# Decoder layer with slot attention and experts: another order of work at the beginning and the end of the self-attention

## The reference

```python
qkv = x @ w_qkv + b_qkv                      # 8 x 256 x 768
att = softmax(where(causal, q @ k.T / 4, -inf))
x = layernorm(x + (att @ v) @ w_proj + b_proj)

Pn = rmsnorm(P, input_norm_w); k_proj = Pn @ Wk.T; v_proj = Pn @ Wv.T
for _ in range(3):                           # slots start as x
    scores = rmsnorm(slots) @ Wq.T @ k_proj.T * SCALE
    attn = softmax(scores, axis=-2)          # over the slots
    attn = attn / (sum(attn, axis=-1) + EPS)
    slots = gru_cell(attn @ v_proj, slots)
x = layernorm(x + slots)
x = layernorm(x + experts(x))                # top 4 of 16
```

## Time and profile before

| | us |
|---|---|
| median of 3 runs | 650.16 |
| lowest and highest | 648.36, 651.65 |
| the profiled execution | 649.62 |
| its span, first to last instruction | 647.9 |

### The profile page before, as it was taken

How to read it: one execution, slowest core, us unless ns; L and a number is a source line. 1 busy time by engine, 2 the same in 40 slices (tenths; PEclk the granted TensorE clock), 3 DMA queues, 4 the chain that set the end, 5 groups by cost and what they waited for, 6 DMA issues and landing times.

```text
span 647.9 us, 13973 instructions
## 1 busy us (share of the span) xinstructions
PE 617.4 (95%) x5064; PEld 562.3 (87%) x5080; DVE 492.4 (76%) x1035; ACT 327.7 (51%) x736; POOL 229.9 (35%) x276
## 2 busy tenths in 40 slices
PE   8889999999989899999999999999999999899996
PEld 7667777787779899999999999999988988899895
DVE  5755677666746888979888798897998987867653
ACT  6334655555764456574556645565456646032220
POOL 9703435243453431332313222232313114262442
PEclk9899999999999999999999999999999999999999
DMA  8545476365200400000000000000000000232250
GB/s 302 173 142 171 144 225 179 114 199 177 60 18 1 163 2 2 17 18 1 0 0 16 16 0 0 0 0 0 0 1 2 2 1 1 70 97 92 75 164 32
DMA packets 31710, 43.34 MB, mean 67 GB/s; under 512 B 3408, under 2 KB 19248, under 8 KB 31664
## 3 DMA queue, kind: packets, MB, share of 16 engines
q1 hardware_dynamic: 31392, 42.47, 20.9%
q10 hardware_dynamic: 272, 0.26, 0.1%
HBM read 29.39 MB, written 13.21 MB: 66 GB/s over the span
## 4 chain that ended last, share of the span: by engine, by line
PE 65%; issue 13%; DVE 13%; POOL 5%; ACT 3%; DMA 1%; another core or an unknown queue 0%; DVEq 0%; POOLq 0%; ACTq 0%
PE bank L450 27%; PE bank L2178 11%; PE bank L1990 4%; PE bank L1890 3%; POOL hid_hl L797 3%; PE bank L1848 2%; PE bank L1855 2%; PE bank L1871 2%; PE bank L458 2%; PE bank L2007 2%; PE bank L1976 1%; PE bank L1875 1%; PE bank L1999 1%; PE bank L1857 1%; PE bank L1920 1%
## 5 line engine op out<-in xcount | busy, mean ns | idle before, releaser
L450 PE MATMUL bank<-slots_hl,whhT_hl 128*128 128x256 f32 x864 | 113.4, 284 | 0.0
L450 PEld LDWEIGHTS bank<-slots_hl,whhT_hl 128*128 128x128 f32 x864 | 105.9, 188 | 2.4 <-ACT gate_z L1106 1.0
L2178 PE MATMUL bank<-attn_hl,vg_hl 128*128 128x256 f32 x864 | 106.9, 281 | 0.9 <-POOL attn_hl L704 0.6
L2178 PEld LDWEIGHTS bank<-attn_hl,vg_hl 128*128 128x128 f32 x864 | 101.6, 188 | 5.5 <-ACT attn_hl L812 4.3
L1298 DVE TENSOR_REDUCE neg_max<-bank 128x2 f32<-128x512 f32 (+1 forms) x96 | 65.5, 690 | 43.3 <-PE bank L1857 29.2
L868 ACT ACTIVATE pT<-bank 128x512 f32<-128x512 f32 x96 | 56.9, 598 | 44.5 <-PE bank L1871 29.0
L689 POOL TENSOR_TENSOR sq<-sq 128x256 f32<-128x256 f32 x24 | 18.1, 754 | 170.9 <-ACT sq L1091 130.4
L675 POOL TENSOR_SCALAR_AFFINE_SELECT pT<-pT 128x512 f32<-128x512 f32 x64 | 40.6, 638 | 103.1 <-ACT pT L868 103.1
L797 POOL TENSOR_TENSOR hid_hl<-hid,hid_hl 128x512 fp32r<-128x512 f32 x32 | 40.9, 1307 | 29.9 <-ACT hid_hl L812 29.9
L450 PE MATMUL bank<-x2T_hl,keys_hl 128*128 128x256 f32 x384 | 48.5, 284 | 0.0
L450 PE MATMUL bank<-values_hl,hid_hl 128*128 128x256 f32 x384 | 48.1, 281 | 0.0
(11 more groups left out here) (219 smaller groups left out, 1299.8 us busy)
## 6 DMA issues: line engine op xcount, KB each, us to landing
gate_rows<-gate_mem SPq DMA_DIRECT2D x48, 128.0 KB, 3.1
q_rows<-q_hl SPq DMA_DIRECT2D x21, 256.0 KB, 2.8
k_rows<-k_hl SPq DMA_DIRECT2D x21, 256.0 KB, 2.6
q_op<-q_rows SPq DMA_DIRECT2D x28, 192.0 KB, 3.1
k_op<-k_rows SPq DMA_DIRECT2D x14, 384.0 KB, 4.3
x_in<-in_x_dram SPq DMA_DIRECT2D x8, 256.0 KB, 3.1
c_in<-in_ctx_dram SPq DMA_DIRECT2D x8, 256.0 KB, 3.3
out_dram<-y_out SPq DMA_DIRECT2D x8, 256.0 KB, 2.8
```

The lines of the kernel that those rows point to most:

```text
L450: mm = pe.matmul(dst, left(a), right(b), start=first and n == 0, stop=last and n == 2, skip_group_check=True)
L2178: mm = pe.matmul(halves(b)[:, m, :], vg_hl[:, j, v_part, 3 * t + r, q:q + P], attn_hl[:, j, at_part, t, :], start=n == 2 and a + m + t == ...
```

## The change

- **Beginning.** Placements 1 to 3 move into the loop on TensorE and VectorE: each stands after the third 0 of the scores (or of their maximum) of the quad before. ScalarE makes the second pair's high part between the copies of placements 1 and 2, no longer in the loop.
- The values of texts 0 and 1 move from the first third of step -4 to its last. The waits for constants and for the first steps' counts move there too.
- On VectorE four small steps on columns (`brz_col` and its neighbours, L1476 to L1480) leave the beginning and stand in step 4, third 1. `W_READ` falls by 4 with them. `FIRST_BESIDE` work now comes after the `key` table's. ScalarE drops its wait for eight such steps.
- On GpSimd the low part of `wproj` moves from before the loop into step -2, behind the texts' low part.
- **End, on ScalarE.** The context's text of step 28 is copied after the heads' sums of step 29. The squares of the first slots move from step 29 to step 30, behind a copy of values. The last heads' sums are copied at the end of step 32, ahead of three copies, no longer at the start of step 33.
- **End, on TensorE.** In step 36 the gates' `hn` products stand before the column sums.

```diff
--- before.py
+++ after.py
@@ -332,7 +332,7 @@
         QUADS_AND_TAIL = range(-LEAD, QUADS + TAIL)
 
 
-        FIRST_BESIDE = {(-4, 0): [("v", 0), ("v", 1)], (-1, 2): [("w", 0)], (0, 2): [("w", 1)], (1, 0): [("w", 2)],
+        FIRST_BESIDE = {(-4, 2): [("v", 0), ("v", 1)], (-1, 2): [("w", 0)], (0, 2): [("w", 1)], (1, 0): [("w", 2)],
                         (1, 2): [("w", 3)], (2, 2): [("w", 4)]}
 
         def beside(quad, third):
@@ -346,7 +346,7 @@
             return work
 
 
-        W_READ = (10, 11, 12, 13, 14)
+        W_READ = (6, 7, 8, 9, 10)
         BESIDE_BANK, BESIDE_FREE = {}, {}
         turn, freed = 0, {6: None, 7: None}
         for quad in QUADS_AND_TAIL:
@@ -721,11 +721,12 @@
                 elif quad == QUADS + 7:
                     attn_lo(-1, UNITS)
 
-            pool.wait_ge(prep_act, 5)
-            pool.tensor_tensor(wproj_hl[:, LO, :, :], st_proj[:, :, :], f32(wproj_hl[:, HI, :, :]), ALU.subtract).then_inc(prep_pool, 1)
-            pool.wait_ge(w_in[4], 16)
             for quad in QUADS_AND_TAIL:
                 period, place = divmod(quad, 8)
+                if quad == -2:
+                    pool.wait_ge(prep_act, 5)
+                    pool.tensor_tensor(wproj_hl[:, LO, :, :], st_proj[:, :, :], f32(wproj_hl[:, HI, :, :]), ALU.subtract).then_inc(prep_pool, 1)
+                    pool.wait_ge(w_in[4], 16)
                 if quad == 0:
                     pool.wait_ge(prep_act, 6)
                     pool.tensor_tensor(whhT_hl[:, LO, :, :], st_hhT[:, :, :], f32(whhT_hl[:, HI, :, :]), ALU.subtract).then_inc(prep_pool, 1)
@@ -961,17 +962,16 @@
                     context_squares(-1, 0)
                 elif quad == QUADS - 6:
                     context_squares(-1, 1)
-                elif quad == QUADS - 4:
-                    context_text_hi(-1, 0, True)
                 elif quad == QUADS - 3:
                     copy(slots_hl[:, 0, HI, :, :], next_text(-1, 0)).then_inc(sl_hi, 1)
                     context_keys_hi(-1, 0, True)
-                    act.activation(sq[:, :, :], next_text(-1, 0), ACT.Square).then_inc(sq_ok, 1)
                 elif quad == QUADS - 2:
                     context_values_hi(-1, 0, 0, True)
+                    act.activation(sq[:, :, :], next_text(-1, 0), ACT.Square).then_inc(sq_ok, 1)
                 elif quad == QUADS - 1:
                     context_values_hi(-1, 0, 1, True)
                 elif quad == QUADS:
+                    heads_out(B - 1, 1)
                     context_values_hi(-1, 0, 2, True)
                     context_text_hi(-1, 1, True)
                     copy(slots_hl[:, 1, HI, :, :], next_text(-1, 1)).then_inc(sl_hi, 1)
@@ -1003,8 +1003,11 @@
             first_operand_hi(1, q_mm, q_hl, bq_col[:, 0:NC], q_hi, 5)
             set_queries(0)
             first_operand_hi(1, k_mm, k_hl, bq_col[:, NC:2 * NC], k_hi, 7)
-            for s in range(1, 4):
-                set_queries(s)
+            set_queries(1)
+            for piece in range(2, 4):
+                text_hi(piece)
+            set_queries(2)
+            set_queries(3)
             act.wait_ge(w_in[7], 16)
             copy(whhT_hl[:, HI, :, :], st_hhT[:, :, :]).then_inc(prep_act, 1)
             act.wait_ge(w_in[8], 32)
@@ -1029,7 +1032,6 @@
                 if quad == 0:
 
                     act.wait_ge(prep_mm, 1)
-                    act.wait_ge(prep_dve, 8)
                     act.wait_ge(prep_pool, 3)
                 for third in range(3):
                     key = place, third
@@ -1039,7 +1041,7 @@
                         keys_hi(2 * period + 2, BESIDE_BANK["k", 2 * period + 2, 0])
                     elif key == (0, 2) and 2 <= 2 * period + 3 < B:
                         keys_hi(2 * period + 3, BESIDE_BANK["k", 2 * period + 3, 0])
-                    elif key == (1, 0) and 0 <= 2 * period - 1 < B:
+                    elif key == (1, 0) and 0 <= 2 * period - 1 < B - 1:
                         heads_out(2 * period - 1, 1)
                     elif key == (2, 2) and 0 <= 2 * period - 1 < B:
                         heads_hi(2 * period - 1)
@@ -1049,11 +1051,10 @@
                         text_out(2 * period - 2)
                     elif key == (4, 2) and 2 <= period + 2 < PAIRS:
                         text_hi(2 * (period + 2))
-                    elif (quad, third) == (-3, 0):
-                        for piece in range(2, 4):
-                            text_hi(piece)
                     elif key == (5, 0) and 0 <= 2 * period < B:
                         heads_out(2 * period, 1)
+                        if quad == QUADS - 3:
+                            context_text_hi(-1, 0, True)
                     elif key == (5, 1) and 2 <= period + 2 < PAIRS:
                         text_hi(2 * (period + 2) + 1)
                     elif key == (6, 1) and 2 <= 2 * period + 4 < B:
@@ -1471,15 +1472,6 @@
             first_operand_lo(1, q_hl, bq_col[:, 0:NC], q_hi, q_lo, 5)
             set_keys(0)
             first_operand_lo(1, k_hl, bq_col[:, NC:2 * NC], k_hi, k_lo, 7)
-            for s in range(1, 4):
-                set_keys(s)
-            step(dve.tensor_tensor(brz_col[:, :], bih_col[:, 0:4], bhh_col[:, 0:4], ALU.add))
-            step(dve.tensor_scalar(brz_col[:, :], brz_col[:, :], 0.5, None, ALU.mult))
-            step(dve.tensor_scalar(bhh_col[:, 2 * NC:], bhh_col[:, 2 * NC:], 0.5, None, ALU.mult))
-
-            step(dve.tensor_scalar(slot_col[:, :], slot_col[:, :], float(D) ** -0.5, None, ALU.mult))
-            dve.wait_ge(w_in[4], 16)
-            dve.wait_ge(consts, 19)
 
             def context_weights_lo(n):
 
@@ -1501,11 +1493,11 @@
                     key = place, third
                     if quad + LEAD < QUADS:
                         maxima(quad + LEAD, third)
-                    for name, n in FIRST_BESIDE.get((quad, third), ()):
-                        if name == "v":
-                            values_out(n, BESIDE_BANK["v", n, 0])
-                        else:
-                            context_weights_lo(n)
+                    if third == 0 and quad + LEAD < 3:
+                        set_keys(quad + LEAD + 1)
+                    if (quad, third) == (-LEAD, 2):
+                        dve.wait_ge(w_in[4], 16)
+                        dve.wait_ge(consts, 19)
                     if key == (0, 0) and 0 <= 2 * period - 2 < B:
                         variance(2 * period - 2)
                     elif key == (0, 1) and 2 <= 2 * period + 2 < B:
@@ -1542,6 +1534,17 @@
                         queries_lo(2 * period + 5, BESIDE_BANK["q", 2 * period + 5, 0])
                     elif key == (7, 2) and 0 <= 2 * period < B:
                         residual(2 * period)
+                    for name, n in FIRST_BESIDE.get((quad, third), ()):
+                        if name == "v":
+                            values_out(n, BESIDE_BANK["v", n, 0])
+                        else:
+                            context_weights_lo(n)
+                    if (quad, third) == (4, 1):
+                        step(dve.tensor_tensor(brz_col[:, :], bih_col[:, 0:4], bhh_col[:, 0:4], ALU.add))
+                        step(dve.tensor_scalar(brz_col[:, :], brz_col[:, :], 0.5, None, ALU.mult))
+                        step(dve.tensor_scalar(bhh_col[:, 2 * NC:], bhh_col[:, 2 * NC:], 0.5, None, ALU.mult))
+
+                        step(dve.tensor_scalar(slot_col[:, :], slot_col[:, :], float(D) ** -0.5, None, ALU.mult))
                 first_context(quad)
 
             def moments(i, chain, per, src, stats, mv, std, var):
@@ -2047,8 +2050,8 @@
                     context_values_of(-1, 1, 1, True)
                     state(-1, UNITS, ("z",), True)
                 elif quad == QUADS + 4:
+                    state(-1, UNITS, ("hn",), True)
                     totals(-1, UNITS, True)
-                    state(-1, UNITS, ("hn",), True)
                 elif quad == QUADS + 5:
                     context_values_of(-1, 1, 2, True)
 
@@ -2114,16 +2117,17 @@
             project_first(5, 1, 0)
             set_rows(0)
             project_first(7, 1, 1)
-            for s in range(1, 4):
-                set_rows(s)
-            pe.wait_ge(prep_dve, 4)
-
-            pe.wait_ge(k_lo, 2)
-            pe.wait_ge(consts, 19)
             for quad in QUADS_AND_TAIL:
                 for third in range(3):
                     if quad + LEAD < QUADS:
                         natural(quad + LEAD, third)
+                    if third == 0 and quad + LEAD < 3:
+                        set_rows(quad + LEAD + 1)
+                    if (quad, third) == (-LEAD, 2):
+                        pe.wait_ge(prep_dve, 4)
+
+                        pe.wait_ge(k_lo, 2)
+                        pe.wait_ge(consts, 19)
                     if 0 <= quad < QUADS:
                         turned(quad, third)
                     if third == 2 and 0 <= quad - 1 < QUADS:
```

## The result

| | us |
|---|---|
| before, median of 20 executions | 649.74 (647.51 to 651.65) |
| after, median of 20 executions | 645.78 (643.14 to 649.66) |
| ratio after / before | 0.9948, 95% interval 0.9935 to 0.9961 |
| profiled execution after (span) | 644.47 (642.8); before 649.62 (647.9) |

A forecast was written before the change was run, and what follows sets the result against it. TensorE, busy 95% of the span, was taken as the bound, with time to win only where it waits or runs slowly. 3.2 + 1.5 - 0.2 + 1.3 + 0.4 = 6.2 us gave 643.9 us, range 641.5 to 648.0.

The forecast's parts named there:

- head, to quad 3's scores: Start of attention on TensorE: quad 3's scores start at 29.05 instead of 32.24 us, gain 3.2 us, some 1.6 of it clock.
- bank wait: TensorE's 1.49 us wait for the second keys to free a PSUM bank goes: gain 1.5 us, bounds 0.8 and 1.5.
- column steps at quad 4: VectorE's four column steps at their new place between maxima cost 0.2 us, bounds 0 and 1.5.
- tail before the sums: End of attention: reordered heads' sums, context copy and square on ScalarE shorten TensorE's waits, gain 1.3 us.
- hidden gate ahead of the column sums: End of attention on TensorE: the hidden gate's 12 products fill a 1.01 us wait, gain 0.4 us.
- the vanished waits on the second keys and on the heads' sums: Signs of being right: TensorE no longer waits on the second keys, nor on the heads' sums before the transposes.
- quad 3 near 29 us: Sign of being right: quad 3's scores, in the head on TensorE, start near 29 us.
- a clock of 1.00: Sign of being right: the granted clock from 26 to 30 us, in the head, reads 1.00.
- the cross phase near 211.3 us: Sign of being right: the first product of the cross phase, after attention, comes near 211.3 us.
- The first rival: Clock falls again in the head, where TensorE still waits: 1.6 us given back, 645.5 us; chance 0.09.
- two others: Bank wait becomes a wait for quad 5's maximum, 645.4 us, chance 0.07; tail edits gain 1.7 us less, 645.6, chance 0.09.
- the operands of the second batch: Rival: they land when they did before, so transfers lose the head's gain and only the tail's is left, 648.4 us; chance 0.07.

The follow-up runs named there:

- e_fill: Changed kernel plus two useless 128x128 products in TensorE's wait before quad 2's scores; ratio to the kernel before 0.9928, 645.60 us at equal clock.
- b_nocols: Kernel before with the four column steps moved from VectorE's head to quad 4, third 1; ratio to the kernel before 1.0007 (0.9985 to 1.0029).
- e_idle: Changed kernel plus two useless maxima on VectorE, lengthening TensorE's waits before quads 2 and 3; ratio to the kernel before 1.0001 (0.9981 to 1.0020).
- e_cols: Changed kernel with the four column steps put back into VectorE's head; ratio to the kernel before 1.0043 (1.0023 to 1.0063).
- e_rowsfill: Changed kernel with the last placement pass before quad 2's scores and two useless products before quad 3's; ratio to the kernel before 0.9953 (0.9928 to 0.9979).
- e_tail: Kernel before with only the edits at the end of attention; ratio to the kernel before 0.9988 (0.9967 to 1.0009).
- e_rowsfirst2: Second run of the changed kernel with the last placement pass before quad 2's scores; ratio to the kernel before 0.9947 (0.9923 to 0.9971), median 645.69 us.
- e_bank: Kernel before with one move on VectorE: second keys' low part ahead of the value weights' low part; ratio to the kernel before 0.9976 (0.9954 to 0.9999).
- e_head: Changed kernel with its whole tail taken back, only the edits at attention's beginning left; ratio to the kernel before 0.9979 (0.9953 to 1.0005).
- r_after: Changed kernel run once more without any edit; ratio to the kernel before 0.9958 (0.9934 to 0.9983).
- r_before: Kernel before run once more without any edit; ratio to its other runs 0.9989 (0.9974 to 1.0004).
- e_rowsfirst: First run of the changed kernel with the last placement pass before quad 2's scores; ratio to the kernel before 0.9925 (0.9901 to 0.9949).

## Why the prediction was right in direction and too large

| term | forecast | pair of traces | what repeats |
|---|---|---|---|
| head, to quad 3's scores | 3.2 | 1.73 | 0.5 |
| bank wait | 1.5 | 1.52 | 1.54 |
| column steps at quad 4 | -0.2 | 0 | 0 |
| tail before the sums | 1.3 | 1.06 | 1.05 |
| hidden gate ahead of the column sums | 0.4 | 0.36 | 0.36 |
| sum | 6.2 | 4.7 | 3.5 |

Of the signs that the prediction named for itself, the vanished waits on the second keys and on the heads' sums came; quad 3 near 29 us, a clock of 1.00 and the cross phase near 211.3 us did not (30.51, 0.57 and 212.86).

- **The head is the mis-sized term.** The walk forward on TensorE was right for an undisturbed head: from the first placement it made 18.05 us to quad 3 (29.05 against 11.00), and e_fill shows 18.22. What failed is the step that followed, the subtraction from 32.24. That number held 1.12 us of the fourth column step, which had met GpSimd's product by 0.04 us, and 1.39 us of low clock. I booked both as removed by the edit: 0.5 + 1.1 + 1.4 and 0.2 of error make the 3.2. The new order does take the steps out of GpSimd's way, but they were caught at a price in one of four traces only, which is worth some 0.3 us on average (1.12 / 4, an estimate; b_nocols does not show it). With it the terms make 3.7 us, and at equal clock 3.65 ± 0.19 were measured. That they meet so closely is in part luck, since the 0.5 and the 0.3 rest on single traces.
- **The clock.** The first rival (1.6 us given back, 645.5) describes the trace after the change and lies near the measured time, but so do two others, and its reason is not the true one: the low stretch is not given back by this change, it comes and goes in both kernels. I had taken the wait of 1.39 us for the cause of the fall, and given the rival 0.09. The clock fell in the head in 11 of 14 traces, first at eight different microseconds from 12 to 27, with that wait, with a shorter one and with none. The Trainium skill (TensorE: Matmul & The Clock Gate, "What's actually happening") has idleness bring the throttle back. e_idle and e_cols lean that way; e_rowsfill, whose clock fell 14 us behind the last wait, is not explained by it, and neither are e_tail (17.2 us), b_nocols (19.1) and e_rowsfirst2 (24.4), where TensorE was busy for all of the 4 us before the fall.
- **The bank wait** went as forecast, down to what is late next: the maximum of quad 5's first scores ends at 45.37 us, 0.06 us ahead of the scores that take its bank.
- **The column steps** cost nothing at quad 4: from quad 3's scores to the first exponentials' wait of the tail TensorE takes 144.42 us with them (after) and 144.46 without (e_bank). One is held there too, in the four traces that I read for it (0.56 to 0.57 us instead of 0.17), but TensorE does not feel it.
- **The tail** was right step by step. The exponentials' wait gained 1.34 us in all (forecast 1.1), and the normalised heads then took 0.3 back by a wait of 0.44 us, the limit that the prediction had named. The cross phase now waits 0.74 us for the attention's high part behind VectorE's weights (L1415), so the swap gave 0.36.
- **No sign of the other rivals.** The first exponential did not wait for GpSimd, which was done 3 us earlier, and the operands of the second batch held nothing up. ScalarE and GpSimd, to be held against the earlier trace rows:

```profile
36.21 0.60 ACT L869 ACTIVATE pT<-bank 128x512 f32<-128x512 f32 x1
...
32.89 0.25 POOL L733 TENSOR_TENSOR eselT_hl<-st_esel,eselT_hl 128x32 fp32r<-128x32 f32 x1
```

## What to carry to other kernels

Before a stretch of one trace is booked as gain, ask which of its numbers would repeat: a tiny operation that takes a microsecond, or a product at half speed, belongs to that execution until a second trace shows it again. A forecast should be the difference of two undisturbed walks, before and after made in the same way, and not a walk subtracted from a measured start. And a step of a few numbers on VectorE is not small beside a long GpSimd fill or product: put it where GpSimd is idle, or behind work that nobody waits for.

## What the runs showed of the hardware

- A stretch at 1.2 GHz costs 1.7 or 3.4 us of work. In the head there was one of the short ones in four traces (before, after, b_nocols, e_rowsfill), one of the long ones in five (e_head, e_tail, r_after, e_idle, e_rowsfirst2), one of each in e_cols, two short and one long in r_before, and none in three (e_bank, e_fill, e_rowsfirst). e_fill and e_cols have one at 551 and 559 us, at the end of a wait of TensorE for VectorE. The same wait, of the same length, is there in the changed kernel, and its clock stayed up (e_fill, then after):

```profile
551.13 0.59 PE L2159 MATMUL bank<-ident,gate 128*16 128x128 f32 x2 [2.23 <-DVE gate L1615]
...
552.85 0.38 PE L2155 MATMUL bank<-ident,gate 128*16 128x128 f32 x2 [2.23 <-DVE gate L1615]
```

- Much of the scatter of the times goes with these stretches: the kernel before ran in 647.6 us on average with a mean clock of 0.996 or more (21 executions) and in 651.3 with 0.990 or less (9). What sets place and number is not settled; waits of 1 us and more seem to make it worse, and are not needed for it.
- The steps of tensor_scalar that met a GpSimd fill or product ended with it, so their length was that of GpSimd's remainder: 0.45, 1.82 and 1.74 us in e_cols, 1.21 and 1.28 in the kernel before.
- The start scatters too: the first placement began between 10.65 (b_nocols) and 13.64 us (e_head), with the same work ahead of it. In e_head TensorE stood for the first weights' low part:

```profile
10.49 2.66 PE L2069 MATMUL bank<-xT_hl,wqkv_hl 128*128 128x256 f32 x20 [2.10 <-DVE wqkv_hl L1236]
```
